# Experts on sorted tokens: seven tiles of 128 instead of four experts over all tokens

## The reference, cut to what matters

```python
h = _layernorm(x, ln_w, ln_b)
logits = h @ router_w
expert_idx = jnp.argmax(logits, axis=-1)
out = jnp.zeros_like(x)
for e in range(E):                      # E = 4
    gv = h @ expert_wv[e]               # 128 -> 1024
    gate_raw, value = jnp.split(gv, 2, axis=-1)
    y = gate_raw * jax.nn.sigmoid(gate_raw) * value @ expert_proj[e]   # 512 -> 128
    out = out + jnp.where((expert_idx == e)[..., None], y, 0.0)
```

## Time and profile before

| | |
|---|---|
| median of three runs | 3768.03 us (3767.74 to 3790.23) |
| profiled execution | 3783.69 us, span 3781.9 us |
| instructions in the trace | 53946 |
| mean granted clock | 0.953 |
| bytes moved by transfers | 65.87 MB, mean 17 GB/s |

### The profile page before, as it was taken

One profiled execution on the slowest core, in us unless ns is written; L12 is line 12 of the kernel. 1 busy time (PEld: TensorE's weight loads), 2 busy tenths in 40 slices (PEclk: granted clock), 3 DMA queues, 4 the chain that ended last, 5 costly groups with the idle time before them and its releaser, 6 DMA issues.

```text
span 3781.9 us, 53946 instructions
## 1 busy us (share of the span) xinstructions
PE 3371.3 (89%) x20319; PEld 1861.5 (49%) x20319; DVE 2505.3 (66%) x5526; ACT 1754.6 (46%) x4156; POOL 380.2 (10%) x676
## 2 busy tenths in 40 slices
PE   2789899999989899999989999998999999998954
PEld 1245455554545555554545545454555545454532
DVE  4555667676776767776776777677676767756453
ACT  0244544545455454545445454545545454554411
POOL 0000100202020010202011020201002020200101
PEclk6799999999999999999999999999999999999965
DMA  4120202020110202020020202001020201100000
GB/s 100 18 29 8 28 2 37 1 37 1 17 22 1 37 2 37 2 30 8 8 31 1 37 1 37 1 11 28 2 37 1 37 1 16 20 1 4 1 3 3
DMA packets 78714, 65.87 MB, mean 17 GB/s; under 512 B 8626, under 2 KB 75124, under 8 KB 78452
## 3 DMA queue, kind: packets, MB, share of 16 engines
q1 hardware_dynamic: 78452, 62.41, 11.5%
HBM read 15.47 MB, written 4.19 MB: 5 GB/s over the span
## 4 chain that ended last, share of the span: by engine, by line
PE 72%; DVE 13%; POOL 6%; ACT 4%; issue 3%; SPq 1%; DMA 1%; POOLq 0%; DVEq 0%; ACTq 0%
PE ps L1376 8%; PE ps L1359 6%; PE ps L1387 6%; PE ps L1394 6%; PE ps L1415 5%; PE ps L1494 5%; PE ps L1479 4%; PE ps L1337 4%; PE ps L1558 4%; DVE nma L1020 3%; PE ps L1580 3%; PE ps L1403 3%; PE ps L1349 3%; PE ps L1460 2%; PE ps L1362 2%
## 5 line engine op out<-in xcount | busy, mean ns | idle before, releaser
L718 ACT ACTIVATE share_a<-ps,nma 128x128 f32<-128x128 f32 (+3 forms) x1024 | 530.2, 523 | 426.4 <-DVE nma L1020 422.4
L1020 DVE TENSOR_REDUCE nma<-ps 128x2 f32<-128x256 f32 (+3 forms) x512 | 420.8, 824 | 426.1 <-PE ps L1362 421.8
L760 ACT ACTIVATE share_z<-ps 128x512 f32<-128x512 f32 (+1 forms) x704 | 368.9, 558 | 419.9 <-PE ps L1481 418.4
L1084 DVE TENSOR_REDUCE nmx<-ps 128x1 f32<-128x384 f32 (+3 forms) x704 | 426.4, 634 | 198.8 <-PE ps L1462 196.1
L614 POOL TENSOR_TENSOR vn<-va,rla 128x512 f32<-128x512 f32 x128 | 133.5, 1043 | 2952.3 <-DVE rla L976 2952.3
L1376 PE MATMUL ps<-share_a,vn 128*64 128x512 f32 (+3 forms) x2048 | 324.0, 462 | 38.5 <-POOL vn L614 37.0
L1460 PE MATMUL ps<-kst,qst 96*128 96x128 bf16 (+3 forms) x1024 | 264.5, 311 | 56.1 <-DMA kst<-part 36.3
L729 ACT ACTIVATE share_g<-ps 128x512 f32<-128x512 f32 x256 | 152.9, 597 | 347.5 <-PE ps L1387 344.5
L1337 PE MATMUL ps<-xnTd,wkqT 128*128 128x512 f32 x512 | 255.2, 622 | 28.2 <-ACT share_a L718 28.2
L1387 PE MATMUL ps<-h2Td,wgv 128*128 128x512 f32 x512 | 268.0, 605 | 2.8 <-ACT share_a L718 2.8
L1394 PE MATMUL ps<-h2Td,wgv 128*128 128x512 f32 x512 | 269.1, 607 | 0.0
(11 more groups left out here) (220 smaller groups left out, 5592.1 us busy)
## 6 DMA issues: line engine op xcount, KB each, us to landing
qst<-part SPq DMA_DIRECT2D x144, 128.0 KB
kst<-part SPq DMA_DIRECT2D x144, 128.0 KB
xin<-in_L_attn_x SPq DMA_DIRECT2D x16, 256.0 KB, 12.6
xk<-xn SPq DMA_DIRECT2D x16, 256.0 KB, 18.5
xres<-in_L_attn_x SPq DMA_DIRECT2D x16, 256.0 KB, 9.9
out<-xn SPq DMA_DIRECT2D x16, 256.0 KB, 11.8
wgv<-in_L_ffn_expert_wv SPq DMA_DIRECT2D x1, 2048.0 KB
qst<-share_h SPq DMA_DIRECT2D x48, 16.0 KB, 2.2
```

The costliest lines, as they stand in the source:

```text
L718: activation(pa[:, h % 4, OFF[t]:OFF[t] + P * (t + 1)], ps[:, b + k, 0:P * (t + 1)], ACT.Exp, bias=nma[:, h, t:t + 1], accum_out=la[:, h, ...
L760: activation(pt[:, n % 2, h % 4:h % 4 + k, 0:wd], src, ACT.Exp, scale=SCALE_B)\
L1020: v.tensor_reduce(nma[:, 2 * p:2 * p + 2, t], ps[:, b:b + 2, 0:P * (t + 1)], AX.X, ALU.max, negate=True).then_inc(amax, 1)
L1084: v.tensor_reduce(nmx[:, h:h + k, t], src, AX.X, ALU.max, negate=True).then_inc(bmax_ready, 1)
```

## The change

Tokens are sorted by expert, each expert's share padded to whole tiles of 128; four experts in 512 tokens need at most seven tiles. Per sequence:

- route's one-hot mask `hot` becomes bf16. rank (TensorE) multiplies it with a strictly triangular matrix and with ones: a token's rank in its expert and the totals. place (VectorE, ten instructions) makes from them each token's row and each tile's expert, as integers.
- scatter (GpSimd) writes the normalised tokens `xh` to their rows of `h_sorted` in device memory, four indirect transfers; SP loads them back as `hs`.
- sort (TensorE) transposes the seven tiles; ScalarE scales them into `hsT`; TensorE loads the seven tiles' experts into registers. h2Td and its copy go.
- gate j and value j now have the tokens of tile j as weights and 512 columns of the tile's expert, addressed by the register, as moving side. turn j transposes the product, ScalarE copies it to `ymT`, down j makes four matmuls, ScalarE copies the result to `ysort`. acc and its mask are gone.
- store_y (ScalarE's queue) writes `ysort` to `y_sorted`, gather (GpSimd) fetches each token's row into `yg`, four indirect transfers, and take_over adds it.
- `ORDER` is new throughout; its second half is below. The pipeline and all other steps are the same but for semaphores. During the start, `h_sorted` is filled with zeros.

```diff
+SORTED = NT + EXPERTS - 1
...
-    ("scores", 7, 2), ("row_max", 43), ("z", 6), ("scores", 7, 3), ("norm", 7), ("shift_rows",), ("mix1", 1),
-    ("gate", 0), ("z", 7), ("load_x",), ("ln0_stats",), ("ln0_root",), ("value", 0), ("gate", 1), ("value",
-    1), ("ao",), ("project1",), ("round_x", 0), ("round_x", 1), ("exps", 0), ("exps", 1), ("add_ao",),
-    ("gate", 2), ("value", 2), ("exps", 2), ("exps", 3), ("ln0_apply",), ("ln1_apply",), ("gate", 3), ("exps",
-    4), ("attend", 0, 0), ("exps", 5), ("exps", 6), ("value", 3), ("gate", 4), ("exps", 7), ("transpose1",),
-    ("value", 4), ("exps", 8), ("exps", 9), ("attend", 0, 1), ("exps", 10), ("attend", 0, 2), ("exps", 11),
-    ("conv",), ("round_x", 2), ("attend", 0, 3), ("exps", 12), ("project", 0, 0), ("gate", 5), ("value", 5),
-    ("round_x", 3), ("round_x", 4), ("exps", 13), ("exps", 14), ("project", 0, 1), ("down", 0), ("exps", 15),
-    ("exps", 16), ("attend", 1, 0), ("exps", 17), ("exps", 18), ("split", 0), ("project", 1, 0), ("gate", 6),
-    ("exps", 19), ("attend", 1, 1), ("exps", 20), ("exps", 21), ("acc", 0), ("value", 6), ("attend", 1, 2),
-    ("exps", 22), ("exps", 23), ("attend", 1, 3), ("project", 1, 1), ("gate", 7), ("exps", 24), ("exps", 25),
-    ("value", 7), ("transpose_xq",), ("gate", 8), ("exps", 26), ("gate1", 0), ("attend", 2, 0), ("exps", 27),
-    ("value", 8), ("up1", 0), ("round_h", 0, 0), ("round_h", 0, 1), ("round_h", 0, 2), ("round_h", 0, 3),
-    ("round_h", 0, 4), ("exps", 28), ("gate", 9), ("value", 9), ("exps", 29), ("exps", 30), ("down", 1),
-    ("gate", 10), ("split", 1), ("transpose_hq", 0), ("exps", 31), ("attend", 2, 1), ("exps", 32), ("attend",
-    2, 2), ("exps", 33), ("attend", 2, 3), ("gate1", 1), ("acc", 1), ("exps", 34), ("exps", 35), ("value",
-    10), ("up1", 1), ("exps", 36), ("round_h", 1, 0), ("round_h", 1, 1), ("round_h", 1, 2), ("round_h", 1, 3),
-    ("round_h", 1, 4), ("gate", 11), ("exps", 37), ("exps", 38), ("attend", 3, 0), ("exps", 39), ("exps", 40),
-    ("exps", 41), ("attend", 3, 1), ("exps", 42), ("exps", 43), ("value", 11), ("attend", 3, 2), ("attend", 3,
-    3), ("gate", 12), ("transpose_hq", 1), ("turn_x",), ("divide", 0), ("divide", 1), ("gate1", 2), ("value",
-    12), ("divide", 2), ("up1", 2), ("divide", 3), ("round_h", 2, 0), ("round_h", 2, 1), ("gate", 13),
-    ("join",), ("round_h", 2, 2), ("round_h", 2, 3), ("round_h", 2, 4), ("value", 13), ("project_y",),
-    ("ln3_stats",), ("down", 2), ("gate", 14), ("transpose_hq", 2), ("acc", 2), ("value", 14), ("gate1", 3),
-    ("gate", 15), ("up1", 3), ("value", 15), ("round_h", 3, 0), ("round_h", 3, 1), ("round_h", 3, 2),
-    ("round_h", 3, 3), ("round_h", 3, 4), ("ln3_root",), ("ln3_apply",), ("down", 3), ("acc", 3),
-    ("transpose_hq", 3), ("down1",), ("transpose3",), ("route",),
...
+    ("row_max", 42), ("scores", 7, 2), ("row_max", 43), ("z", 6), ("scores", 7, 3), ("shift_rows",), ("norm",
+    7), ("mix1", 1), ("z", 7), ("sort",), ("project1",), ("round_x", 0), ("load_x",), ("ln0_stats",), ("exps",
+    0), ("exps", 1), ("ln0_root",), ("ln0_apply",), ("ln1_apply",), ("ao",), ("add_ao",), ("gate", 0),
+    ("value", 0), ("gate", 1), ("exps", 2), ("exps", 3), ("value", 1), ("round_x", 1), ("turn", 0),
+    ("round_x", 2), ("round_x", 3), ("round_x", 4), ("exps", 4), ("attend", 0, 0), ("exps", 5), ("exps", 6),
+    ("down", 0), ("gate", 2), ("exps", 7), ("transpose1",), ("value", 2), ("exps", 8), ("exps", 9), ("turn",
+    1), ("attend", 0, 1), ("exps", 10), ("attend", 0, 2), ("exps", 11), ("attend", 0, 3), ("conv",), ("exps",
+    12), ("project", 0, 0), ("down", 1), ("exps", 13), ("exps", 14), ("project", 0, 1), ("split", 0), ("gate",
+    3), ("exps", 15), ("exps", 16), ("attend", 1, 0), ("exps", 17), ("value", 3), ("exps", 18), ("project", 1,
+    0), ("turn", 2), ("exps", 19), ("attend", 1, 1), ("exps", 20), ("exps", 21), ("project", 1, 1), ("split",
+    1), ("attend", 1, 2), ("exps", 22), ("exps", 23), ("attend", 1, 3), ("transpose_xq",), ("down", 2),
+    ("gate", 4), ("gate1", 0), ("exps", 24), ("exps", 25), ("value", 4), ("turn", 3), ("up1", 0), ("exps",
+    26), ("round_h", 0, 0), ("round_h", 0, 1), ("round_h", 0, 2), ("round_h", 0, 3), ("attend", 2, 0),
+    ("exps", 27), ("exps", 28), ("round_h", 0, 4), ("down", 3), ("gate", 5), ("value", 5), ("exps", 29),
+    ("turn", 4), ("exps", 30), ("exps", 31), ("attend", 2, 1), ("down", 4), ("transpose_hq", 0), ("gate", 6),
+    ("gate1", 1), ("value", 6), ("turn", 5), ("up1", 1), ("round_h", 1, 0), ("exps", 32), ("down", 5),
+    ("turn", 6), ("attend", 2, 2), ("exps", 33), ("attend", 2, 3), ("round_h", 1, 1), ("down", 6),
+    ("store_y",), ("round_h", 1, 2), ("round_h", 1, 3), ("round_h", 1, 4), ("exps", 34), ("exps", 35),
+    ("transpose_hq", 1), ("exps", 36), ("exps", 37), ("gate1", 2), ("exps", 38), ("attend", 3, 0), ("exps",
+    39), ("up1", 2), ("exps", 40), ("exps", 41), ("attend", 3, 1), ("exps", 42), ("exps", 43), ("attend", 3,
+    2), ("attend", 3, 3), ("turn_x",), ("round_h", 2, 0), ("round_h", 2, 1), ("round_h", 2, 2), ("round_h", 2,
+    3), ("round_h", 2, 4), ("transpose_hq", 2), ("gather",), ("divide", 0), ("divide", 1), ("gate1", 3),
+    ("divide", 2), ("divide", 3), ("up1", 3), ("round_h", 3, 0), ("round_h", 3, 1), ("round_h", 3, 2),
+    ("round_h", 3, 3), ("join",), ("project_y",), ("round_h", 3, 4), ("transpose_hq", 3), ("ln3_stats",),
+    ("ln3_root",), ("ln3_apply",), ("down1",), ("transpose3",), ("route",), ("rank",), ("place",),
+    ("scatter",),
 ]
...
+                def load_sorted():
+                    sp.wait_ge(scattered, count(i, AHEAD["scattered"], 16 * NT))
+                    sp.dma_start(hs, h_sorted.rearrange("(t p) c -> p t c", p=P)).then_inc(hs_loaded, 16)
...
+                def scatter():
+                    pool.wait_ge(placed, count(nxt, AHEAD["placed"], 1))
+                    if type(nxt[0]) is not int or nxt[0] + nxt[1]:
+                        pool.wait_ge(scatter_turn, count(nxt, AHEAD["scatter_turn"], 0))
+                    if i is not None:
+                        pool.wait_ge(hs_loaded, count(i, DENSE["hs_loaded"], 16))
+                    nc.gpsimd.tensor_tensor(turn_s[:, :], vones[0:1, VCOLS - 1:VCOLS],
+                                            vones[0:1, VCOLS - 1:VCOLS], ALU.mult).then_inc(scatter_turn, 1)
+                    for t in range(NT):
+                        nc.gpsimd.indirect_dma_start(
+                            h_sorted, bass.IndirectOffsetOnAxis(place_i[:, t:t + 1].bitcast(U32), 0),
+                            xh[:, t, :], None).then_inc(scattered, 16)
+
+                def gather():
+                    pool.wait_ge(y_stored, count(i, DENSE["y_stored"], 16))
+                    if type(i[0]) is not int or i[0] + i[1]:
+                        pool.wait_ge(gather_turn, count(i, DENSE["gather_turn"], 0))
+                    nc.gpsimd.tensor_tensor(turn_g[:, :], vones[0:1, VCOLS - 1:VCOLS],
+                                            vones[0:1, VCOLS - 1:VCOLS], ALU.mult).then_inc(gather_turn, 1)
+                    for t in range(NT):
+                        nc.gpsimd.indirect_dma_start(
+                            yg[:, t, :], None, y_sorted,
+                            bass.IndirectOffsetOnAxis(placed_d[:, t:t + 1].bitcast(U32), 0)).then_inc(y_gathered, 16)
...
+                def turn(j):
+                    act.wait_ge(yT_psum, count(i, DENSE["yT_psum"], j + 1))
+                    if j >= 2:
+                        act.wait_ge(down_psum, count(i, DENSE["down_psum"], j - 1))
+                    copy(ymT[:, j % 2, :, :].rearrange("p c t -> p (c t)"), ps[:, GATE_BANK[j % 2], :])\
+                       .then_inc(yT_ready, 1)
+
+                def down(j):
+                    act.wait_ge(down_psum, count(i, DENSE["down_psum"], j + 1))
+                    copy(ysort[:, j, :], ps[:, VALUE_BANK[j % 2], 0:C]).then_inc(y_ready, 1)
+
+                def store_y():
+                    act.wait_ge(y_ready, count(i, DENSE["y_ready"], SORTED))
+                    if prv is not None:
+                        act.wait_ge(y_gathered, count(prv, DENSE["y_gathered"], 16 * NT))
+                    act.dma_start(y_sorted.rearrange("(t p) c -> p t c", p=P), ysort).then_inc(y_stored, 16)
...
-                    dve.wait_ge(hot_ready, count(i, AHEAD["hot_ready"], 1))
+                    dve.wait_ge(placed, count(i, AHEAD["placed"], 1))
                     if prv is not None:
-                        dve.wait_ge(moe_acc, count(prv, DENSE["moe_acc"], EXPERTS))
+                        dve.wait_ge(down_psum, count(prv, DENSE["down_psum"], SORTED))
                         dve.wait_ge(behind_step, count(prv, BEHIND_STEPS, 1))
-                    v.tensor_copy(hotd[:, :, :], hot[:, :, :])
+                    v.tensor_copy(placed_d[:, :], place_i[:, :])
+                    v.tensor_copy(expert_d[:, 0:SORTED], expert_i[:, 0:SORTED])
...
+                def place():
```

(89 more changed lines are left out.)

234 lines of the change are left out of this document (128 added, 106 removed), and 14 rows, old and new, of the table ORDER.

## The result

The changed kernel takes 3818.8 us (median of 4 runs, 3818.2 to 3820.9), the kernel before, beside it, 3776.7 (3767.7 to 3790.2): a ratio of 1.011, 95% interval 1.007 to 1.015. It is slower by about 1%, where 1.5% less time was forecast (3711 us against 3768).

A forecast was written before the change was run, and what follows sets the result against it. TensorE bounds only the middle stretch, a VectorE-shared chain the end; 4.1 + 1.7 - 1.7 = 4.1 us a round, 61 in 15, less about 4 for the pipeline's fill, gives -57: 3711 us against 3768.0, range 3670 to 3755.

The forecast's parts named there:

- Middle stretch: Last mix to second gate1 in each round: 60.9 us before, 56.8 after, a gain of 4.1.
- Loads: Seven register loads behind sort in the middle stretch: 0.5 us each, less 0.4 of cover, 3.1 a round.
- Register addresses at nothing: 42 matmuls a round with addresses from a register: no cost, hidden by work queued on TensorE.
- End stretch: Second gate1 to the next first key projection, bound by a chain: 38.4 us against 40.1, a gain of 1.7.
- Clock: Gaps in the new end stretch bring one more stretch of half speed a round, costing 1.7 us.
- First stretch: First key projection to last mix, 116.0 us: same TensorE work in a new order, no change, plus or minus 4.5.
- the sign that it was wrong: The prediction calls itself wrong if the first stretch moves by over 5 us.
- Route and rank on the path: End of a round: route's 1.9 us and rank's 0.6 now stand ahead of the next first key projection.
- Place, take_over, scatter and gather hidden: Around the round's start: place (2.1 us), the dearer take_over, scatters and gathers run beside other work and cost nothing.
- the rival of the late gather: Store and gathers take over 34 us, so take_over waits; at 41, 7 us a round, 3816 us; chance 0.18.
- The change gives nothing: Each of 42 register-addressed matmuls comes 0.1 us late, 4.2 a round: 3774 us; loads of 1.0 nearly the same; chance 0.15.
- The gain is kept: Loads hidden, no clock loss: 3638 us; half the first stretch's idle time closed too: 3571; named 3605; chance 0.22.

The follow-up runs named there:

- e5: Changed kernel with the seven register loads moved from behind sort to ahead of scores (4,0): 3734.0 us, ratio 0.990.
- e17: Changed kernel with 14 register loads instead of seven at the same place, each value loaded twice: 3931.9 us, ratio 1.039.
- e2: Changed kernel without its register loads and with fixed expert addresses (tile j uses expert j mod 4): 3727.0 us, ratio 0.985.
- e1: Changed kernel with ten extra matmuls a round, never read, in the gaps of the end stretch: 3750.3 us, ratio 0.9915.
- e11: Changed kernel with the old first-stretch order, ten extra matmuls in the end stretch and an own buffer for the block's output: 3696.2 us, ratio 0.977.
- e10: Changed kernel with loads ahead of scores (4,0), first key projection ahead of rank and eight extra matmuls: 3658.7 us, ratio 0.967.
- e4: Changed kernel with the old order from take_over to the last mix, without gate 0: 3754.2 us, ratio 0.992.
- e6: Changed kernel with the next round's first key projection ahead of rank on TensorE: 3749.6 us, ratio 0.992.
- e12: e8 with an own buffer for the block's output and the register loads directly behind kq 5: 3632.1 us, ratio 0.960.
- e14: e12 with four more extra matmuls, in the first stretch: 3609.8 us, ratio 0.955.
- e7: Changed kernel with the old first-stretch order and ten extra matmuls in the end stretch: 3761.9 us, ratio 0.997.
- e8: Changed kernel with old first-stretch order, loads ahead of scores (4,0), first key projection ahead of rank and eight extra matmuls: 3791.2 us, ratio 1.003.

## Why the prediction was wrong, step by step

**The account.** It forecast 4.1 us a round less; in the eleven rounds of the table it is 1.5 more. Over the whole span: the first round starts 4.8 us later (4 was forecast), 15 rounds of 1.43 make 21.4, and what follows the last round's first key projection is 8.3 longer (351.2 against 342.9; nothing was forecast for it). Together 34.6, the difference of the spans.

**Middle stretch: right.** 56.8 was forecast, 56.4 measured, a gain of 4.4 for 4.1. Its parts hold in sum only. Work and order: 53.7 forecast, 53.0 in e5. Loads: 3.1 forecast and 3.4 measured, by another road (the gap, forecast at 3 to 4 us, is 1.7): 0.64 us each and not 0.5, 2.8 us of them covered by what was queued and not 0.4, and the rest doubled by the half clock that follows the gap. The Trainium skill (DMA: Bandwidth & Descriptors, Latency and other measured facts) puts a register load at 600 ns or more; e17 agrees, and the nearest row, a DMA issue on SP, was the poorer guide.

**Register addresses at nothing: right.** e2 and e5 have the same middle and end.

**End stretch: the chain right, its clock wrong.** 38.4 was forecast, 19.4 for two FFN tiles and 19.0 from the fourth gate1 on. In e1, at nearly full clock, the two parts are 19.6 and 18.9, and from the fourth gate1 to down1 it takes 9.7, as in the kernel before. In the changed kernel they are 20.7 and 19.9, at a clock of 0.86.

**Two terms failed, of about the same size: the clock's price and the first stretch's "no change".**

**Clock: mis-sized.** The mechanism was named, its price too low. The forecast took one more stretch of half speed a round, 1.7 us, from a place where TensorE had been busy two thirds of the time. In the changed kernel there are up to five: behind the loads, ahead of and behind the last rounding step, across the start of the round, and, in four of eleven rounds, around scores (3,0) for 12 us and more. The kernel before has one there as well, in nine of eleven rounds, of 3 to 7 us. Full clock in the end alone gave back 2.0 there and 2.4 in the first stretch behind it (e1), 4.4 for the 1.7 forecast. That is 2.7 of the 5.6 by which the round missed; the clock lost behind the loads is a further 1.7, which stands in the middle's sum above. The other 2.9 are the first stretch's own loss, 3.2, less the 0.3 by which the middle did better.

**First stretch, no change plus or minus 4.5: wrong.** It lost 5.6, more than the 5 that the prediction had named as the sign that it was wrong. Its order was new, and the prediction gave the new order no cost, with no reason but that TensorE's work in it was the same. Of the loss 2.4 is the clock handed on by the end (e1). The remaining 3.2 is the new order: with the old one in its place (e11 against e1) the stretch is 3.3 shorter at the same granted clock, and has the 116.8 of the kernel before. Moving the loads and the first key projection doesn't bring it back (e10: 120.1 from the first key projection on). Which steps of the new order cost it stays open. e4 could not show this, since its first stretch swings between 117.8 and 128.6 by the store and the clock together.

**Route and rank on the path: right.** e6 takes 4.4 a round out, for the 2.5 forecast and the clock on top.

**Place, take_over, scatter and gather hidden: right.** e11 has the first stretch of the kernel before, 116.8. The gathers are issued from 1906.47 to 1911.25 and take_over, which needs them, follows place at once, 27 us later:
```profile
1906.47 1.02 POOL L724 DMA_INDIRECT yg<-y_sorted,placed_d  x1 [0.15 <-issue]
...
1938.58 0.17 DVE L1258 CAST expert_i<-expert_f 128x7 int32<-128x7 f32 x1
1938.69 0.69 DVE L1266 TENSOR_TENSOR xp<-xacc,yg 128x512 f32<-128x512 f32 x1
```
So the rival of the late gather is false although its time, 3816, was nearly met: a time that fits proves no mechanism. Its bounds were too wide because the store of 448 KB was priced by a load issued right behind the stack loads; that load lands in 4.1 us in the changed kernel, where it is issued later, and not in 12.6, and the store landed in 3.0 us. The Trainium skill (SBUF — State Buffer, SBUF: two separate sides) warns that VectorE can keep GpSimd's descriptors out; here an indirect transfer's issue took 0.94 to 1.02 us with VectorE busy two thirds of the stretch, so no run shows it. "The change gives nothing" was the case nearest in kind, but its reasons, dear addresses and loads of 1.0 us, are both false. "The gain is kept", 3571 to 3638, was reached only by e12 and e14, with the costs of loads, clock, route and store taken away and the old order in the first stretch.

**What was not thought of:** the store of the output. The last exps moved 7 us nearer to the round's end, and with them 23 us of stack loads on SP and the store behind them. In the changed kernel the new order of the first stretch had room for it, since ln2_apply is due 26 us into the round there and 12 us in the old order, which had not (e4, e7).

## What to carry to other kernels

When work is taken from an engine that was full, ask what the new gaps do to its clock before counting the gain: here ten matmuls of no use made a kernel almost 2% faster. Fill or close all gaps, since half speed removed in one place can come back in the next. When steps are put in a new order, price the new order by itself: here it cost as much as the clock. A register load is priced by what stands in the queue ahead of it, so put a batch of them behind long matmuls, never behind a wait. And when a cure that worked alone fails beside another, look for a resource that the first one reaches earlier: here a buffer that was still being stored.

## What the runs showed of the hardware

- TensorE was granted either 2.4 or 1.2 GHz, with no other level in any trace here. A gap of 1.7 us behind sort was followed by half speed in nine of eleven rounds of e1 and by none in two (middle 56.4 or 54.8), with the same instructions. The down1 of 12 matmuls (24 records) takes 2.94 us at the one level and 4.83 across both.
- A register load from memory takes TensorE's sequencer 0.64 us (14 against 7: 6.23 - 1.73 = 4.50). 4.7 us of matmuls since the last wait hid seven of them (e5), 4.2 us left a gap of 0.39 (e12), 0.4 us one of 4.2 (e8).
- Matmuls with an operand whose address comes from a register ran as those with fixed ones (603 and 593 ns a record against 605; same stages in e2 and e5).
- An indirect transfer of 128 rows of 512 bytes keeps GpSimd for 0.94 to 1.02 us in the round shown, with 0.3 us between two, and four of them take 4.8 us (1906.47 to 1911.25 for the gathers).
